# Attention weighing issued once a step, 512 queries wide, in place of two halves of 256

## The reference, cut to what matters

```python
q, k, v = proj(wq, bq), proj(wk, bk), proj(wv, bv)      # 16 heads of 16 channels
scores = jnp.einsum('bhqd,bhkd->bhqk', q, k) / np.sqrt(HEAD_DIM)
attn = jax.nn.softmax(scores + bias[None], axis=-1)     # bias by relative position
out = jnp.einsum('bhqk,bhkd->bhqd', attn, v)
```

## Time and profile before

| | |
|---|---|
| median of 3 runs | 3169.09 us (3157.96 to 3169.86) |
| profiled execution: own time, span in the trace | 3172.75 us, 3171.0 us |
| PE busy (weight loads apart) | 2918.3 us, 92% |
| DVE busy | 2051.0 us, 65% |
| ACT busy | 1731.9 us, 55% |
| POOL busy | 1253.0 us, 40% |
| mean granted TensorE clock | 0.956 of full |

### The profile page before, as it was taken

How to read it: one execution, slowest core, us unless ns; L and a number is a source line. 1 busy time by engine, 2 the same in 40 slices (tenths; PEclk the granted TensorE clock), 3 DMA queues, 4 the chain that set the end, 5 groups by cost and what they waited for, 6 DMA issues and landing times.

```text
span 3171.0 us, 51535 instructions
## 1 busy us (share of the span) xinstructions
PE 2918.3 (92%) x18786; PEld 1518.0 (48%) x18786; DVE 2051.0 (65%) x4319; ACT 1731.9 (55%) x3667; POOL 1253.0 (40%) x1764
## 2 busy tenths in 40 slices
PE   5979999899998999989999899988999989998997
PEld 3643356433564336643466434653346533465334
DVE  4459735796457954579545795458944589345992
ACT  2418834388343873448634486435854358533684
POOL 2325533255332553335433354333543335433453
PEclk8979999899998999989999899998999989999899
DMA  6041000500005000150001400023000330004100
GB/s 171 1 106 15 2 1 1 133 15 2 1 13 121 15 2 1 22 113 15 1 1 31 103 15 1 1 53 81 15 1 1 73 62 15 1 1 98 36 2 14
DMA packets 54779, 107.58 MB, mean 34 GB/s; under 512 B 12400, under 2 KB 34976, under 8 KB 54400
## 3 DMA queue, kind: packets, MB, share of 16 engines
q1 hardware_dynamic: 54272, 104.22, 14.5%
q10 hardware_dynamic: 256, 0.07, 0.0%
HBM read 56.66 MB, written 36.72 MB: 29 GB/s over the span
## 4 chain that ended last, share of the span: by engine, by line
PE 70%; DVE 11%; DMA 5%; SPq 4%; issue 4%; POOL 3%; ACT 3%; ACTq 1%; POOLq 0%; DVEq 0%
PE psum L733 18%; PE psum L782 15%; PE psum L551 11%; DVE mx L1448 6%; PE psum L759 4%; PE psum L833 4%; SPq L446 3%; DMA SQ<-mrow 2%; PE psum L586 2%; PE psum L882 2%; PE psum L814 2%; PE psum L868 2%; PE psum L622 2%; DMA parts<-mixed 2%; PE psum L885 2%
## 5 line engine op out<-in xcount | busy, mean ns | idle before, releaser
L1448 DVE TENSOR_REDUCE mx<-psum 128x1 f32<-128x512 f32 x2048 | 1263.3, 684 | 160.3 <-PE psum L733 158.0
L1191 ACT ACTIVATE Z<-psum 128x512 f32<-128x512 f32 x2048 | 1117.8, 597 | 312.5 <-PE psum L759 281.0
L1644 POOL TENSOR_TENSOR Z<-Z,band_exp 128x256 f32<-128x256 f32 (+1 forms) x1152 | 713.3, 641 | 806.9 <-ACT Z L1191 800.5
L733 PE MATMUL psum<-SK,SQ 63*128 63x512 f32 x2048 | 817.9, 484 | 55.0 <-DVE mx L1448 31.4
L759 PE MATMUL psum<-SQ,SK 64*128 64x512 f32 x2048 | 781.0, 461 | 48.2 <-DMA SQ<-mrow 48.2
L782 PE MATMUL psum<-Z,Vx 128*17 128x256 f32 x8192 | 639.6, 386 | 0.1
L733 PEld LDWEIGHTS psum<-SK,SQ 63*128 63x128 f32 x2048 | 340.6, 196 | 506.5 <-DVE mx L1448 375.7
L551 PE MATMUL psum<-Wqkvg,Z 128*128 128x512 f32 x768 | 381.5, 622 | 18.6 <-ACT Z L1086 18.6
L759 PEld LDWEIGHTS psum<-SQ,SK 64*128 64x128 f32 x2048 | 320.2, 189 | 121.5 <-ACT Z L1191 56.8
L782 PEld LDWEIGHTS psum<-Z,Vx 128*17 128x17 f32 x8192 | 138.2, 95 | 353.7 <-issue 289.3
L1589 POOL TENSOR_TENSOR Z<-Z 128x512 f32<-128x512 f32 x64 | 81.2, 1269 | 358.8 <-DVE Z L1370 358.8
(11 more groups left out here) (121 smaller groups left out, 3241.2 us busy)
## 6 DMA issues: line engine op xcount, KB each, us to landing
parts<-Z SPq DMA_DIRECT2D x32, 512.0 KB
X<-L_attn_a_x SPq DMA_DIRECT2D x8, 1024.0 KB, 5.5
SQ<-parts SPq DMA_DIRECT2D x32, 256.0 KB, 7.8
SK<-parts SPq DMA_DIRECT2D x32, 256.0 KB, 10.1
SQ<-parts SPq DMA_DIRECT2D x16, 512.0 KB, 8.2
SK<-parts SPq DMA_DIRECT2D x16, 512.0 KB, 13.1
out<-X SPq DMA_DIRECT2D x16, 512.0 KB, 18.5
SQ<-mixed SPq DMA_DIRECT2D x96, 64.0 KB, 2.3
```

Of the source, the lines that this page charges most:

```text
L733: pe.matmul(row_bank(c), SQ[rows_of(h, MAX_ROW), h // 2, i * P:i * P + P], SK[rows_of(h, MAX_ROW), h // 2, 512 * k:512 * k + 512], start=T ...
L1191: nc.scalar.activation(ring[:, n % RING, :], col_bank(n), ACT.Exp)\
L1448: nc.vector.tensor_reduce(mx2[:, blk % 2, col, k:k + 1], row_bank(2 * u + k), AX_X, ALU.max)\
L1644: nc.gpsimd.tensor_tensor(ring[:, n % RING, a:z], ring[:, n % RING, a:z], band_exp[:, 4 * hg + COLS[i], at:at + z - a], ALU.mult)\
```

## The change

The weighing of a step is one group of four matmuls (one for each head) over all 512 queries. It stands where the first half stood, behind the first two pairs of the step; the second half, behind the last two pairs, is gone. The semaphore e_pv, which says that a step is weighed, is raised there too. Banks, ring, LAG and all other engines' programs stay.

```diff
-            def weigh(b, s, part):
+            def weigh(b, s):
 
                 hg, half, j = step(s)
-                if part == 0:
-                    if bands[s]:
-                        need(pe, e_band, b, 4 * banded[s])
-                    else:
-                        need(pe, e_p, b, 4 * s + 4)
-                    if s % 8 == 0:
-                        need(pe, mx_row, b, s // 8 + 1)
-                cols = slice(256 * part, 256 * part + 256)
+                if bands[s]:
+                    need(pe, e_band, b, 4 * banded[s])
+                else:
+                    need(pe, e_p, b, 4 * s + 4)
+                if s % 8 == 0:
+                    need(pe, mx_row, b, s // 8 + 1)
                 for c in range(4):
-                    mm = pe.matmul(sum_bank(s // 8)[32 * c:32 * c + HD + 1, cols], Vx[:, j, 4 * hg + c, :],
-                                   ring[:, (4 * s + COLS.index(c)) % RING, cols],
-                                   start=s % 8 == 0 and part == 0, stop=s % 8 == 7, skip_group_check=True)
-                if part == 1:
-                    mm.then_inc(e_pv.sem, 1)
+                    mm = pe.matmul(sum_bank(s // 8)[32 * c:32 * c + HD + 1, :], Vx[:, j, 4 * hg + c, :],
+                                   ring[:, (4 * s + COLS.index(c)) % RING, :],
+                                   start=s % 8 == 0, stop=s % 8 == 7, skip_group_check=True)
+                mm.then_inc(e_pv.sem, 1)
...
                     if s >= LAG:
-                        weigh(b, s - LAG, 0)
+                        weigh(b, s - LAG)
                     if s < NS:
                         for k in range(2):
                             if u + 1 < NU:
                                 score_rows(b, u + 1, k)
                             score_cols(b, s, 2 + k)
-                    if s >= LAG:
-                        weigh(b, s - LAG, 1)
```

## The result

The changed kernel takes 3222.28 us (median of 4 runs, 3218.43 to 3229.32) against 3169.48 us for the kernel before (median of 4 runs, one more than in the table ahead of the prediction): 52.8 us more, a ratio of 1.0174 with a 95% interval of 1.0142 to 1.0207. The forecast was 3234, slower.

A forecast was written before the change was run, and what follows sets the result against it. PE's own pace, 2.44 us a step, was taken to bound the kernel, with DVE close at 2.39. The terms summed to 8.14 us a batch, 65 us over eight batches, giving 3234 us, range 3200 to 3272.

The forecast's parts named there:

- PE alone would be faster: PE's own pace in an ordinary step with one weighing, without bank waits: 2.08 us against 2.44.
- The wide weighing costs 0.98: One 512-query weighing a step takes 0.98 us, with bounds of 0.56 and 1.12.
- Rival 1: Saved change-overs are kept, needing a whole weighing under 0.73 us: -63 us, 3106 us; chance 0.08.
- The ring: Fourth pair after a weighing waits for DVE to release the first pair's bank: 2.69 us an ordinary step, against 2.44.
- the columns' ring: Same wait in steps without rows, over ACT's exponentials: 2.62 us a step against 2.44, +0.19.
- The specials of a block: Extras per eight steps: output transposes +0.20, DVE's normalisation +0.52, maximum transposes 0; block 22.24 us against 21.09.
- Steps 3 to 5: Three steps ahead of a batch's blocks, each 2.69 us, against 7.57 together: +0.5 a batch.
- The tail: Steps without rows ending a batch: six ordinary ones at +0.19, the rest 0; +1.14 us a batch.
- The signs: Expected profile: steps 2.69 us with rows, DVE idle 0.3 a step, PE busy well under 20.7 a block, clock 1.00.
- rival 2: A draw: whole weighing 0.7 to 0.8 us, or banks released some 0.2 earlier; 3169 us, chance 0.07.
- rival 3: More is lost: special steps stay at 1.6 a block, or the weighing costs 1.12; 3275 to 3300 us, chance 0.06.
- rival 4: The clock falls inside the loop, costing about 70 us more: 3305 us; chance 0.03.

The follow-up runs named there:

- e3: Changed kernel with each row maximum over 256 of 512 keys and each exponential over 256 of 512 queries; 3082.76 us, ratio 0.9739.
- e6: Kernel before with halves up to step 53, then the whole weighing, with six banks for columns in steps 54 to 59; 3142.07 us, ratio 0.9921.
- e1: Changed kernel with the weighing again as two groups of 256 queries, back to back where the whole one stands; ratio 1.0199.
- e8: Changed kernel with the whole weighing behind the last two pairs of the step instead of the first two; 3280.96 us, ratio 1.0359.
- e2: Changed kernel with each row maximum taken over the first 256 of 512 keys; 3171.6 us, ratio 1.0013.
- e9: Changed kernel with two banks in turn for the rows in place of three; 3476.6 us, one run.
- e10: Kernel before, weighing in halves, with two banks in turn for the rows in place of three; 3356.0 us, one run.

## Why the prediction was right

- **PE alone would be faster.** Right in kind: the weighing's union fell by 96 us. In steps with rows its size, 2.08, was never seen, since a ring closes in every ordinary one (2.42 at the least, e3); P1 to P3 do come at the 0.34 and 0.23 that the estimate took. For steps without rows 2.08 is wrong: it counts four pairs where there are four columns, and these run two at a time, so PE alone takes 1.65 (e6).
- **The wide weighing costs 0.98.** 0.99 measured (1453.45 to 1454.44). Rival 1, which needed 0.73, fell on this and on the next point.
- **The ring.** 0.53 + 0.75 + 0.43 + 0.98 = 2.69 predicted, 2.69 to 2.70 measured in ordinary steps with rows. e1 takes the width out and changes nothing, and neither does the place in e8. In e2 the step stops at the columns' ring (2.62 by the sum, 2.62 measured). In e3 it follows the shortened exponential (2.40 by the sum with its measured 0.38, 2.42 measured). e9 and e10 take a bank away and come out at the sums written before they ran. The cause is shown.
- **The specials of a block.** +0.20 for the output transposes: steps 18 and 19 take 3.37 + 2.21 = 5.58 against 2 x 2.69. +0.52 for the normalisation: steps 20 to 22 take 3.41 + 2.79 + 2.39 = 8.59 against 8.07. The maximum transposes came out at nothing, as predicted. The block is 22.26, predicted 22.24.
- **Steps 3 to 5.** +0.8 in place of +0.5: the maximum transposes in step 5 are not hidden there (3.00), but step 6 gives it back (2.39), in the next block.
- **The tail.** This term was mis-sized: +1.14 a batch predicted, 0.00 measured. I let the columns' ring close in six steps and put the rest at nothing. It closes in 55 to 57 (2.59, +0.16 each). Steps 58 and 60, with transposes and projections, lose 0.48 and 0.47 more. Steps 54, 59 and 62, where a break lies in or ahead of the run, take 2.06, 1.98 and 1.98, which together is 1.3 us less than before, and step 61 gains 0.13. What the prediction had not seen is how much a whole weighing gains where no bank is waited for. That gains and losses cancel to 0.00 is chance.
- **The sum.** The five blocks cost 5.83 a batch (5.75 predicted), steps 46 to 53 0.76 (0.75). In all 8.14 a batch predicted, 7.40 measured in the loop, 59 us instead of 65. The rest of the distance to 52.8 lies outside the loop, in waits for DMA that vary by execution; I did not separate it further.
- **The signs.** Two were read too loosely. DVE idles 0.21 a step, not 0.30: the last of its four maxima takes 0.68 and not 0.60. And PE's busy time in a block was to be well under 20.7; it is 20.69, as good as before (20.73). A part of each wait is hidden in the records: P4 came 0.49 later than the estimated 0.22 behind P3, and only 0.32 of it shows as idle time. So this number cannot tell a PE that streams from one that waits.
- **Rivals 2 to 4** did not come about. The weighing takes 0.99, neither 0.7 to 0.8 (rival 2) nor 1.12 (rival 3), a bank is held 1.28, and the block has no more than the predicted specials. The clock did not fall inside the loop (rival 4): in batch 3 it is 1.00 from 1416 to 1583 us. Only the first steps are below that (0.50 in the first 4.7 us), and they are so in the kernel before too (0.61). The 3285 given for half of rival 3's excess takes both of its excesses together, 5 and 8 us a batch; half of either one is 3254 to 3266.

## What to carry to other kernels

Before a bursty order is judged by how it fills TensorE, add up how long a buffer is held, from the load of the matmul that fills it to the matmul that may follow its reader, and lay that against the distance between the first and the last use in a burst: here 1.28 us against 0.77. An order that puts the consumer's work between the producer's bursts in smaller parts hides the hold, at the price of more change-overs. Where buffers are idle for a stretch (here three banks in the last ten steps), give them to the burst there, and use the order that fits each stretch.

## What the runs showed that I had not expected

- A maximum over half the row takes 0.42 us, not half of 0.68, and an exponential over half of it 0.38, not half of 0.60. By these two widths some 0.16 us of either is a fixed part that narrower work doesn't shorten (an estimate).
- Without rows, a run of four column scores takes 0.67 us, as long as a run of two of one parity (0.66), because it keeps both halves of the array at work. With six banks PE then needs 1.65 us a step, less than the 1.96 of ACT's four exponentials (20 of them take 9.91 us without a break).
- The hold of a bank hardly varies: from P1's load to the pair that waited for its bank 1.28 us in the changed kernel (1451.74 to 1453.02), 1.28 in e9, 1.29 in e8. The two steps with two row banks came out by hand to 0.02 us.
